# Ordering TensorE's work in the attention loop of a four-layer graph network: row sums behind the counts, transposes and picks later

## The chip, the cores and the metric

The kernel runs on one core of one Trainium2 chip. The metric is the device time of one execution in microseconds. The core's engines work at the same time, each through its own queue in order: TensorE (PE; its weight loads stand apart as PEld), VectorE (DVE), ScalarE (ACT), GpSimd (POOL) and SyncE (SP). They wait for one another by semaphores only.

## What is computed

A graph of 3125 nodes with 64 features and 100000 edges sorted by destination goes through four layers, each added to its input and normalised. The change touches the first, a graph attention over 8 relations:

```python
def _gat_relation(x, src, dst, mask, N, Wr, a_src, a_dst, br):
    h = x @ Wr
    s = h @ a_src
    d = h @ a_dst
    e = jax.nn.leaky_relu(s[src] + d[dst], negative_slope=NEG_SLOPE)
    e = jnp.where(mask, e, -jnp.inf)
    m = jax.ops.segment_max(e, dst, num_segments=N)
    w = jnp.where(mask, jnp.exp(e - m[dst]), 0.0)
    denom = jax.ops.segment_sum(w, dst, num_segments=N)
    alpha = w / denom[dst]
    msg = alpha[:, None] * h[src]
    return jax.ops.segment_sum(msg, dst, num_segments=N) + br
```

The other three layers (degree-normalised sums, three message steps, an edge network) run behind it and are not changed.

## The kernel before

The attention takes the sorted edges in visits of 128 edges. A visit serves one group of 16 nodes, that is 128 (node, relation) pairs. Eight visits (`B`) make a batch, and `NB0` = 122 batches the stage. Each engine runs a `step(n)` for each batch, unrolled by 6 (`RING`) inside a loop (`turns`), and in one step it works on several batches: `n.has(d)` guards the work on batch n+d.

In step n, for each batch concerned:

- SyncE loads the records of batch n+4, and GpSimd gathers the table rows of the batch's source nodes with eight indirect DMAs (line 828). The gather of batch n waits for `hw_ready` of batch n-6, because there are six buffers.
- VectorE (from line 995 on) reduces the transposed scores of batch n to their maxima (`top`, line 1023), makes the masked scores `far` of batch n+1 (line 1031, needs the gathered rows and the `hit` activations of batch n-1), does a chain of small operations, builds the one-hot operands of batch n+2 (lines 1092 to 1101), and then interleaves three things: eight updates of the accumulator with the row sums of batch n-2 (line 1012), eight one-hot `pair_hot` operations for batch n+2 (line 1004, the last sets `hot_ready`), and the weighted rows `hw` of batch n-1 (line 1122).
- TensorE carries a running count table into PSUM (`carries`, line 957, two matmuls) and then adds eight visits to it one after the other (`counts`, line 966, called counts 0 to 7 here). Each count may start only when ScalarE has copied the table as the visit before left it. Between the counts stand the rest of TensorE's work: eight row sums of batch n-2 (`gather_sums`, line 938, two passes each in float32), eight transposes of `far` of batch n+1 (`scores`, line 911) and eight small matmuls that pick values for batch n (`picks`, line 924).
- ScalarE copies each count to SBUF (`keep`, line 864, keeps 0 to 7), and between the copies computes `weight` of batch n-1 (line 878), `fade` of batch n (line 887), the two halves of `hit` for batch n (`hits`, line 856) and the two halves of `hit_t` for batch n+1 (`turned`, line 846). Behind keep 7 it issues the store of the eight copies (line 869).

The order on each engine is written out by hand in its `step`. So TensorE and ScalarE hand a table back and forth eight times a batch, in one PSUM bank: a count, its keep, the next count.

Of the kernel before, what the change touches and what calls it, by code (L numbers as in the profile page):

```python
# [6 lines left out]
ACT = mybir.ActivationFunctionType  # L7
# [695 lines left out]
def attention(nc, k):  # L703
# [5 lines left out]
    with Stage(nc) as c:  # L709
# [6 lines left out]
        def sem(name):  # L716
# [21 lines left out]
        fade_in = sb("fade_in", [P, 2, B])  # L738
        fade = sb("fade", [P, 3, B])
# [15 lines left out]
        hit_ready, hit_t_ready, fade_asked, fade_ready = (sem("hit_ready"), sem("hit_t_ready"), sem("fade_asked"),  # L755
                                                          sem("fade_ready"))
# [79 lines left out]
        @block.scalar  # L836
        def _(act):
            a = nc.scalar

            def turned(n, d, h):  # L840

                s, half = (n.o + d) % 2, slice(4 * h, 4 * h + 4)
                act.wait_ge(masked_ready, n(2, 2 * d + h + 1))
                if h == 0 and n.after(2 - d):
                    act.wait_ge(picked_ready, n(1, d - 1))
                a.activation(hit_t[:, s, half], masked[:, half], ACT.Identity, bias=k.ones_f[:, 0:1],
                             scale=1.0 / BIG).then_inc(hit_t_ready, 1)

            def hits(n, h):

                s, half = n.o % 2, slice(4 * h, 4 * h + 4)
                if h == 0:
                    act.wait_ge(far_ready, n(1, 1))
                    if n.after(2):
                        act.wait_ge(sums_ready, n(1, -1))
                a.activation(hit[:, s, half], far[:, s, half], ACT.Identity, bias=k.ones_f[:, 0:1],
                             scale=1.0 / BIG).then_inc(hit_ready, 1)

            def keep(n, d, i):

                if i == 0 and n.after(2 - d):
                    act.wait_ge(count_written[(n.o + d) % 2], n.pairs(d) * 16)
                act.wait_ge(near_ready, n(B, d * B + i + 1))
                a.copy(count[:, (n.o + d) % 2, i, 0:AW], near[:, (n.o + d) % 2, 0:AW]).then_inc(count_ready, 1)  # L864

            def store(n, d):

                act.wait_ge(count_ready, n(B, d * B + B))
                act.dma_start(k.slots[:, bass.ds(n(B, d * B), B), :], count[:, (n.o + d) % 2, 0:B]
                              ).then_inc(count_written[(n.o + d) % 2], 16)  # L870

            def step(n):
                if n.has(1):
                    keep(n, 1, 0)
                    keep(n, 1, 1)
                if n.has(-1):
                    act.wait_ge(weight_asked, n(1))
                    a.activation(weight[:, (n.o + 1) % 2], lz[:, (n.o + 1) % 2], ACT.Exp).then_inc(weight_ready, 1)
                if n.has(1):
                    keep(n, 1, 2)  # L880
                if n.has(0):
                    hits(n, 0)
                if n.has(1):
                    keep(n, 1, 3)
                if n.has(0):
                    act.wait_ge(fade_asked, n(1, 1))
                    a.activation(fade[:, n.o % 3], fade_in[:, n.o % 2], ACT.Exp).then_inc(fade_ready, 1)
                if n.has(1):
                    keep(n, 1, 4)
                if n.has(0):  # L890
                    hits(n, 1)
                if n.has(1):
                    keep(n, 1, 5)
                    turned(n, 1, 0)
                    keep(n, 1, 6)
                    turned(n, 1, 1)
                    keep(n, 1, 7)
                    store(n, 1)

            turns(act, -1, step)  # L900

        @block.tensor
        def _(pe):
            def scores(n, d, h):

                if h == 0:
                    pe.wait_ge(far_ready, n(1, d + 1))
                    if n.after(1 - d):
                        pe.wait_ge(top_ready, n(1, d))
                for u in range(4 * h, 4 * h + 4):  # L910
                    t = pe.transpose(masked[:, u, :], far[:, (n.o + d) % 2, u, :], k.ident[:])  # L911
                t.then_inc(masked_ready, 1)

            def picks(n, h):

                s = n.o % 2
                if h == 0:
                    pe.wait_ge(pick_ready, n(1, 1))
                    pe.wait_ge(hit_t_ready, n(2, 2))
                    if n.after(1):  # L920

                        pe.wait_ge(zed_taken, n(1))
                for u in range(4 * h, 4 * h + 4):
                    m = pe.matmul(picked[:, 6 * u:6 * u + 6], hit_t[:, s, u, :], pick[:, s, :, u], start=True, stop=True)
                if h == 1:
                    m.then_inc(picked_ready, 1)

            def gather_sums(n, d, h):

                s = (n.o + d) % 2  # L930
                if h == 0:
                    pe.wait_ge(hw_ready, n(1, d + 1))
                    pe.wait_ge(hit_ready, n(2, 2 * d + 2))
                    if n.after(1 - d):

                        pe.wait_ge(acc_step, n(B, d * B))
                for u in range(4 * h, 4 * h + 4):
                    m = pe.matmul(sums[:, u // 4, (u % 4) * TW:(u % 4 + 1) * TW], hit[:, s, u, :], hw[:, s, u, :],  # L938
                                  start=True, stop=True)
                if h == 1:  # L940
                    m.then_inc(sums_ready, 1)

            def carries(n, d):

                s, past = (n.o + d) % 2, (n.o + d + 1) % 2
                _, at = nc.values_load_multi_w_load_instructions(
                    k.start_row[0:1, bass.ds(n(1, d), 1), 0:2].rearrange("a p c -> a (p c)"),
                    engines=[mybir.EngineType.PE], min_val=0, max_val=B,
                    skip_runtime_bounds_check_because="a visit of a batch, or the zeros behind it")
                if n.after(1 - d):  # L950
                    pe.wait_ge(count_ready, n(B, d * B))
                    if n.after(2 - d):
                        pe.wait_ge(deg_added, n(1, d - 1))
                else:
                    pe.wait_ge(run_start, 5)
                for i in range(2):
                    pe.matmul(near[:, s, 0:SW], k.carry_by[:, i, :],
                              count[:, past, bass.ds(at[i], 1), :].rearrange("p i c -> p (i c)"), start=(i == 0), stop=False)

            def counts(n, d, i):  # L960

                s = (n.o + d) % 2
                if i:

                    pe.wait_ge(count_ready, n(B, d * B + i))
                pe.matmul(near[:, s, 0:SW], low_hot[:, s, i, :], pair_hot[:, s, i, :], start=False,  # L966
                          stop=True, skip_group_check=(i > 0)).then_inc(near_ready, 1)

            def step(n):
                if n.has(1):  # L970
                    carries(n, 1)
                    pe.wait_ge(hot_ready, n(1, 2))
                    counts(n, 1, 0)
                if n.has(-2):
                    gather_sums(n, -2, 0)
                if n.has(1):
                    counts(n, 1, 1)
                if n.has(-2):
                    gather_sums(n, -2, 1)
                if n.has(1):  # L980
                    counts(n, 1, 2)
                    scores(n, 1, 0)
                    counts(n, 1, 3)
                    scores(n, 1, 1)
                    counts(n, 1, 4)
                if n.has(0):
                    picks(n, 0)
                if n.has(1):
                    counts(n, 1, 5)
                if n.has(0):  # L990
                    picks(n, 1)
                if n.has(1):
                    counts(n, 1, 6)
                    counts(n, 1, 7)

            turns(pe, -1, step)

        @block.vector
# [696 lines left out]
def keep(nc, k):  # L1695

    with Stage(nc) as c:
        kept = c.semaphore("kept")
        block = c.enter_context(nc.Block())

        @block.vector
        def _(dve):
            nc.vector.tensor_copy(k.x_skip[:], k.x_n[:]).then_inc(kept, 1)
            dve.wait_ge(kept, 1)
# [637 lines left out]
```

## Time and profile before

| | |
|---|---|
| median of 3 runs | 4369.33 us (4359.36 to 4374.9) |
| the profiled execution | 4391.71 us, its span 4390.0 us |
| attention, first `top` to last `top` | 274.8 to 2005.0 us |
| busy over the whole span | PE 67%, PEld 46%, DVE 59%, ACT 34%, POOL 55% |

The page of the profile gives busy tenths of each engine in 40 slices of 110 us; slices 3 to 18 are the attention. Groups of instructions stand by line, engine and operation, with their busy time and with the idle time of the engine before them, together with what ended it. A timeline lists instructions in order of start. "Issue" and "remote" in brackets name idle time for which the profile shows no engine that ended it.

### The profile page before, as it was taken

To read this page: it belongs to the slowest core of one execution; us is meant where nothing else is said; L and a number is where in the kernel's file an instruction comes from. 1 tells how busy PE (TensorE), PEld (TensorE's weight loads), DVE (VectorE), ACT (ScalarE), POOL (GpSimd) and SP (SyncE) were. 2 spreads that over 40 slices of the span, in tenths; PEclk is the share of its full clock that TensorE was granted. 3 is DMA by queue.
4 is the path that set the end of the run, shared out by engine and by line. 5 is a ranking of instruction groups with operands and counts; after the bars stand their busy time and mean duration, and the time that the engine had idled before them with its cause. 6 is when DMAs were issued, how large, how long until landed. Compare 5 with 4: busy or idle time off the path is not lost. (4 is left out here: it accounts for less than half of the span.)

```text
span 4390.0 us, 76379 instructions
## 1 busy us (share of the span) xinstructions
PE 2941.5 (67%) x16134; PEld 2027.4 (46%) x16135; DVE 2594.5 (59%) x9305; ACT 1475.1 (34%) x3181; POOL 2417.1 (55%) x1836
## 2 busy tenths in 40 slices
PE   1636666666666666656567785887878878778762
PEld 0324544444444454443232332666656666666541
DVE  6148888888888887776954443444344443444422
ACT  0124444444444444443010000443333333333320
POOL 0056666666666666550000000588888888888881
PEclk9955555555555555556778876888988989899876
DMA  1353333333333333782603230455555555555543
GB/s 43 100 125 98 97 95 102 97 97 108 90 97 97 106 98 89 86 103 98 169 25 86 71 93 4 47 54 54 53 54 53 54 54 53 54 54 53 54 43 74
DMA packets 654307, 338.20 MB, mean 77 GB/s; under 512 B 437168, under 2 KB 614627, under 8 KB 653284
## 3 DMA queue, kind: packets, MB, share of 16 engines
q0 software_dynamic: 148736, 86.57, 20.5%
q1 hardware_dynamic: 487814, 143.62, 15.5%
q10 hardware_dynamic: 17568, 106.20, 6.0%
q14 instruction: 157, 1.29, 0.1%
q8 instruction: 32, 0.52, 0.1%
HBM read 158.05 MB, written 202.84 MB: 82 GB/s over the span
## 5 line engine op out<-in xcount | busy, mean ns | idle before, releaser
L1847 POOL DMA_INDIRECT sums<-el_rows,el_idx x816 | 1269.2, 1555 | 782.2 <-DVE el_rows L2061 533.9
L828 POOL DMA_INDIRECT at_hs<-table,at_rec_s x976 | 1140.3, 1168 | 614.9 <-DVE at_hw L1122 310.3
L966 PE MATMUL near_ps<-at_pair_hot,at_src_low_hot 128*128 128x425 f16 x976 | 507.4, 520 | 580.1 <-ACT at_count_s L864 319.8
L864 ACT CAST at_count_s<-near_ps 128x400 f16<-128x400 f32 x976 | 481.9, 494 | 987.5 <-PE near_ps L966 446.0
L2059 DVE CAST el_idx<-el_place 128x4 uint32<-128x4 f32 x204 | 35.3, 173 | 840.6 <-DMA sums<-el_rows,el_idx 791.8
L938 PEld LDWEIGHTS sums_ps<-at_hw,at_hit 128*128 128x128 f32 x1952 | 472.9, 334 | 36.3 <-issue 31.7
L966 PEld LDWEIGHTS near_ps<-at_pair_hot,at_src_low_hot 128*128 128x128 f16 x976 | 135.4, 139 | 722.8 <-ACT at_count_s L864 397.9
L938 PE MATMUL sums_ps<-at_hw,at_hit 128*128 128x66 f32 x1952 | 442.2, 408 | 8.7 <-DVE acc L1012 8.7
L1409 PE MATMUL sum_total<-chunk,sum_parts 128*128 128x512 f16 (+1 forms) x700 | 264.2, 391 | 119.9 <-DVE chunk L1511 98.3
L1004 DVE TENSOR_SCALAR at_pair_hot<-iota_wide,at_rec_s 128x400 f16<-128x400 f16 x976 | 324.7, 335 | 0.0
L1995 ACT ACTIVATE el_h<-el_h_ps,el_valid 128x128 f32<-128x128 f32 x816 | 232.6, 368 | 239.3 <-PE el_h_ps L1909 175.8
L1012 DVE SCALAR_TENSOR_TENSOR acc<-acc,at_fade,sums_ps 128x66 f32 x976 | 269.4, 276 | 68.6 <-remote 42.0
L1511 DVE SCALAR_TENSOR_TENSOR chunk<-chunk,minus_past 128x400 f16<-128x400 f16 x464 | 254.3, 625 | 88.0 <-DMA chunk<-slots 88.0
L1863 PE MATMUL el_miss_t<-ident_b,el_miss 128*128 128x128 bf16 x816 | 83.9, 264 | 305.1 <-DVE el_miss L2033 305.1
L1023 DVE TENSOR_REDUCE at_top<-masked 128x8 f32<-128x1024 f32 x122 | 149.1, 1222 | 221.4 <-issue 137.0
L1411 PE MATMUL sum_total<-chunk,sum_parts 128*128 128x512 f16 (+1 forms) x700 | 262.6, 388 | 0.0
L911 PE MATMUL masked<-ident,at_far 128*128 128x128 f32 x976 | 248.6, 407 | 2.7 <-DVE at_far L1031 1.9
L1920 PE MATMUL el_sum_ps<-el_h,el_join 128*128 128x128 f32 x1632 | 245.0, 298 | 7.4 <-DVE el_rows L2061 4.9
L1985 ACT ACTIVATE el_h<-el_h_ps,b 128x512 f32<-128x512 f32 x204 | 140.2, 687 | 318.4 <-PE el_h_ps L1898 264.9
L1031 DVE SCALAR_TENSOR_TENSOR at_far<-at_miss,at_hs 128x1024 f32<-128x1024 f16 x122 | 240.3, 1970 | 0.0
L1909 PE MATMUL el_h_ps<-w,el_h 128*128 128x128 f32 x1632 | 237.3, 289 | 0.0
L1895 PE MATMUL el_h_ps<-el_ea_t,w1b 64*128 64x512 f32 x408 | 235.0, 656 | 0.2 <-issue 0.2
(339 smaller groups left out, 5095.2 us busy)
## 6 DMA issues: line engine op xcount, KB each, us to landing
slots<-at_count_s ACTq DMA_DIRECT2D x122, 850.0 KB
chunk<-slots SPq DMA_DIRECT2D x480, 100.0 KB
el_rec<-attr SPq DMA_DIRECT2D x816, 32.0 KB
attr<-in_edge_attr SPq DMA_DIRECT2D x19, 1248.0 KB
at_rec_s<-meta SPq DMA_DIRECT2D x992, 3.5 KB
at_hs<-table,at_rec_s POOLq DMA_INDIRECT x976
el_pair<-meta SPq DMA_DIRECT2D x816, 1.0 KB
sums<-el_rows,el_idx POOLq DMA_INDIRECT x816
```

Source lines behind the costliest of these rows:

```text
L828: pool.indirect_dma_start(hs[:, s, u, :], None, k.table, bass.IndirectOffsetOnAxis(rec[:, s, u, 0:1].bitcast(U32), 0)).then_inc(gathered[s ...
L864: a.copy(count[:, (n.o + d) % 2, i, 0:AW], near[:, (n.o + d) % 2, 0:AW]).then_inc(count_ready, 1)
L911: t = pe.transpose(masked[:, u, :], far[:, (n.o + d) % 2, u, :], k.ident[:])
L938: m = pe.matmul(sums[:, u // 4, (u % 4) * TW:(u % 4 + 1) * TW], hit[:, s, u, :], hw[:, s, u, :], start=True, stop=True)
L966: pe.matmul(near[:, s, 0:SW], low_hot[:, s, i, :], pair_hot[:, s, i, :], start=False, stop=True, skip_group_check=(i > 0)).then_inc(near_r ...
L1004: return v.tensor_scalar(pair_hot[:, (n.o + d) % 2, u, 0:AW], k.iota_wide[:], rec[:, (n.o + d) % RING, u, 5:6], None, ALU.is_equal)
L1012: v.scalar_tensor_tensor(a, a, fade[:, (n.o + d) % 3, u:u + 1], sums[:, u // 4, (u % 4) * TW:(u % 4 + 1) * TW], ALU.mult, ALU.add).then_in ...
L1409: pe.matmul(first, parts[:, t, 0:2, :].rearrange("p i d -> p (i d)"), near, start=(t == 0), stop=(degree and t == NT - 1))
L1411: m = pe.matmul(second, parts[:, t, 2:4, :].rearrange("p i d -> p (i d)"), near, start=(degree and t == 0), stop=(t == NT - 1))
L1511: ins = v.scalar_tensor_tensor(at, k.chunk[:, q % HELD, g - 1, :], k.minus_past[:, q * CG + g - 1:q * CG + g], at, ALU.mult, ALU.add)
L1847: pool.indirect_dma_start(k.sums_flat[a], bass.IndirectOffsetOnAxis(idx[:, j, a:a + 1], 0), rows[:, j, a, :], None, compute_op=ALU.add).th ...
L1920: m = pe.matmul(sum_ps[:, j % 2, u * P:(u + 1) * P], join[:, s, 4 * h + u, :], h2[:, j % 2, u, :], start=True, stop=True)
```

## The change

Only the orders written out by hand in the attention's TensorE and ScalarE steps change; no instruction is added or removed. On TensorE the eight row sums, formerly four behind count 0 and four behind count 1, stand two behind each of counts 0 to 3. The two halves of the transposes, formerly behind counts 2 and 3, stand behind counts 4 and 5; the two halves of the picks, formerly behind counts 4 and 5, stand behind counts 6 and 7. On ScalarE keeps 0 to 3 come in a row, then `weight`, keep 4, the first half of `hit`, keep 5, the first half of `hit_t`, keep 6, its second half, keep 7 and the store; the second half of `hit` and `fade` come last, behind the store.

```diff
@@ ScalarE
             def step(n):
                 if n.has(1):
-                    keep(n, 1, 0)
-                    keep(n, 1, 1)
+                    for i in range(4):
+                        keep(n, 1, i)
                 if n.has(-1):
                     act.wait_ge(weight_asked, n(1))
                     a.activation(weight[:, (n.o + 1) % 2], lz[:, (n.o + 1) % 2], ACT.Exp).then_inc(weight_ready, 1)
                 if n.has(1):
-                    keep(n, 1, 2)
+                    keep(n, 1, 4)
                 if n.has(0):
                     hits(n, 0)
-                if n.has(1):
-                    keep(n, 1, 3)
-                if n.has(0):
-                    act.wait_ge(fade_asked, n(1, 1))
-                    a.activation(fade[:, n.o % 3], fade_in[:, n.o % 2], ACT.Exp).then_inc(fade_ready, 1)
-                if n.has(1):
-                    keep(n, 1, 4)
-                if n.has(0):
-                    hits(n, 1)
                 if n.has(1):
                     keep(n, 1, 5)
                     turned(n, 1, 0)
...
                     turned(n, 1, 1)
                     keep(n, 1, 7)
                     store(n, 1)
+                if n.has(0):
+                    hits(n, 1)
+                    act.wait_ge(fade_asked, n(1, 1))
+                    a.activation(fade[:, n.o % 3], fade_in[:, n.o % 2], ACT.Exp).then_inc(fade_ready, 1)
@@ TensorE
-                for u in range(4 * h, 4 * h + 4):
+                for u in range(2 * h, 2 * h + 2):
                     m = pe.matmul(sums[:, u // 4, (u % 4) * TW:(u % 4 + 1) * TW], hit[:, s, u, :], hw[:, s, u, :],
                                   start=True, stop=True)
-                if h == 1:
+                if h == 3:
                     m.then_inc(sums_ready, 1)
...
-                if n.has(-2):
-                    gather_sums(n, -2, 0)
+                for h in range(4):
+                    if n.has(-2):
+                        gather_sums(n, -2, h)
+                    if n.has(1):
+                        counts(n, 1, h + 1)
                 if n.has(1):
-                    counts(n, 1, 1)
-                if n.has(-2):
-                    gather_sums(n, -2, 1)
-                if n.has(1):
-                    counts(n, 1, 2)
                     scores(n, 1, 0)
-                    counts(n, 1, 3)
+                    counts(n, 1, 5)
                     scores(n, 1, 1)
-                    counts(n, 1, 4)
+                    counts(n, 1, 6)
                 if n.has(0):
                     picks(n, 0)
                 if n.has(1):
-                    counts(n, 1, 5)
+                    counts(n, 1, 7)
                 if n.has(0):
                     picks(n, 1)
-                if n.has(1):
-                    counts(n, 1, 6)
-                    counts(n, 1, 7)
```

## Rows read from the trace of the kernel before

**Rows 1.** The page's 40 slices of the span: busy tenths, and the granted clock in tenths.
```profile
DVE  6148888888888887776954443444344443444422
ACT  0124444444444444443010000443333333333320
POOL 0056666666666666550000000588888888888881
PEclk9955555555555555556778876888988989899876
```

**Rows 2.** Line 1023 up to 1840 us: count, min/median/max ns, first and last start.
```profile
L1023 DVE TENSOR_REDUCE at_top<-masked x111: 1203/1225/1226, 274.8 to 1832.7; 128x8 f32<-128x1024 f32 x111
```

**Rows 3.** Timeline of one step: start us, us, engine, line, operation, [idle before <-releaser].
```profile
839.03 1.23 DVE L1023 TENSOR_REDUCE at_top<-masked 128x8 f32<-128x1024 f32 x1 [2.31 <-issue]
...
840.29 0.56 PE L966 MATMUL near_ps<-at_pair_hot,at_src_low_hot 128*128 128x425 f16 x1
...
840.65 1.81 PE L938 MATMUL sums_ps<-at_hw,at_hit 128*128 128x66 f32 x8
840.89 0.50 ACT L864 CAST at_count_s<-near_ps 128x400 f16<-128x400 f32 x1 [1.43 <-issue]
...
842.25 0.56 PE L966 MATMUL near_ps<-at_pair_hot,at_src_low_hot 128*128 128x425 f16 x1
...
845.42 0.56 PE L966 MATMUL near_ps<-at_pair_hot,at_src_low_hot 128*128 128x425 f16 x1
...
846.63 0.56 PE L966 MATMUL near_ps<-at_pair_hot,at_src_low_hot 128*128 128x425 f16 x1
846.69 0.28 DVE L1012 SCALAR_TENSOR_TENSOR acc<-acc,at_fade,sums_ps 128x66 f32 x1
...
847.63 0.49 ACT L864 CAST at_count_s<-near_ps 128x400 f16<-128x400 f32 x1 [1.01 <-PE near_ps L966]
...
850.14 0.50 ACT L864 CAST at_count_s<-near_ps 128x400 f16<-128x400 f32 x1
...
850.51 0.71 ACT L846 ACTIVATE at_hit_t<-masked,ones_f 128x512 bf16<-128x512 f32 x1
...
850.69 0.54 PE L966 MATMUL near_ps<-at_pair_hot,at_src_low_hot 128*128 128x425 f16 x1 [0.62 <-ACT at_count_s L864]
851.27 0.49 ACT L864 CAST at_count_s<-near_ps 128x400 f16<-128x400 f32 x1
...
851.91 0.36 ACTq L869 DMA_DIRECT2D slots<-at_count_s  x1
...
852.59 0.56 PE L966 MATMUL near_ps<-at_pair_hot,at_src_low_hot 128*128 128x425 f16 x1
```

**Rows 4.** Timeline of VectorE over one step in which it never waits.
```profile
1631.55 1.23 DVE L1023 TENSOR_REDUCE at_top<-masked 128x8 f32<-128x1024 f32 x1 [2.52 <-issue]
...
1642.95 0.43 DVE L1004 TENSOR_SCALAR at_pair_hot<-iota_wide,at_rec_s 128x400 f16<-128x400 f16 x1
1643.29 1.20 DVE L1023 TENSOR_REDUCE at_top<-masked 128x8 f32<-128x1024 f32 x1
```

**Rows 5.** Timeline around one long idle time of ScalarE between a count and its keep.
```profile
997.60 0.56 PE L966 MATMUL near_ps<-at_pair_hot,at_src_low_hot 128*128 128x425 f16 x1
...
1002.02 0.49 ACT L864 CAST at_count_s<-near_ps 128x400 f16<-128x400 f32 x1 [4.83 <-remote]
```

**Rows 6.** Waits, 800 to 1600 us: waiter <- releaser: us in total, times, longest.
```profile
POOL at_hs L828 <- DVE at_hw L1122: 137.7, 44, 7.4
ACT at_count_s L864 <- remote: 136.2, 35, 6.1
...
DVE acc L1012 <- remote: 21.1, 17, 2.9
```

**Rows 7.** GpSimd's gathers: their group, 800 to 1600 us (busy us, mean ns | idle), and one from the timeline.
```profile
L828 POOL DMA_INDIRECT at_hs<-table,at_rec_s x452 | 533.5, 1180 | 267.9 <-DVE at_hw L1122 137.7 <-issue 130.2
...
840.61 2.38 POOL L828 DMA_INDIRECT at_hs<-table,at_rec_s  x1 [0.30 <-issue]
```

## The prediction

> **What bounds the kernel now.** I read the slices first. In slices 3 to 18, the attention, no engine is full: VectorE stands at eight tenths, ScalarE at four, GpSimd at six, with TensorE's clock mostly near its lower level of 1.2 GHz [rows 1]. A loop in which nobody is full is bound by a hand-over, so the next question is how long a step lasts and who waits in it. The starts of `top` give the step: 110 steps from 274.8 to 1832.7 us, 14.16 us each [rows 2]. The last eleven, up to 2005.0, are slower still (15.7 us each), and I claim nothing there.
>
> What a step could last on VectorE alone is seen where it never waits: from 1631.55 to the next `top` at 1643.29 are 11.74 us [rows 4]. So on average 2.4 us of a step are VectorE waiting. For whom? The timeline of an ordinary step shows the loop between TensorE and ScalarE [rows 3]. From count 0 of one batch (840.29) to count 0 of the next (852.59) it takes 12.30 us and is closed: count, keep, next count, and after keep 7 the carry and count 0 again. Its parts are uneven. Count 0 to keep 0 takes 0.60 (840.29 to 840.89), and a keep to the next count 0.55 (850.14 to 850.69), so a link costs 1.15 where nothing else stands in it. But count 1 comes 1.96 behind count 0 (842.25 against 840.29), because four row sums of two passes fill the 1.81 us between them, and TensorE takes its queue in order. Count 2 is another 1.96 behind, for the same reason. Counts 2 to 4 are 1.21 apart (845.42 to 846.63), counts 4 to 7 together take 4.06 (846.63 to 850.69), and count 7 to the next count 0 takes 1.90.
>
> The second thing in the loop is ScalarE standing still. In 800 to 1600 us, 56.5 steps, it was idle before a keep 35 times with no engine named as releaser, 136.2 us in all [rows 6], 3.9 us each and 0.62 a step. In the one shown, the count began at 997.60, its keep was due at 998.20 and came at 1002.02 [rows 5]: 3.8 us lost. As part of such idle time is ordinary waiting, I take 3.3 us for an average one. Nothing in the chain hides it today: 12.30 + 0.62 x 3.3 = 14.35, against 14.16 measured. That sum is my test that the chain is what sets the step.
>
> **The change, part by part.** *Row sums.* Eight sums stay eight, at about 0.45 us each (four in 1.81). Two behind a count take 0.9, which together with the count's own 0.35 (840.29 to the first sum at 840.65) makes 1.25 at most; by the starts, four sums and a count take 1.96, so two take 1.96 - 0.84 = 1.12. ScalarE's link of 1.15 runs at the same time. So four gaps of 1.15 (at most 1.25) replace 1.96 + 1.96 + 1.21 + 1.21: 4.6 for 6.34, a gain of 1.7 us.
>
> *Transposes.* A count with four transposes is the 1.21 gap seen above. They move to gaps 4 to 5 and 5 to 6: 2.42. *Picks.* These are short and lie within a link: gap 6 to 7 is 1.15, and the second half lies behind count 7, beside keep 7. So counts 4 to 7 take 3.57 instead of 4.06; half a microsecond of that 4.06 is keep 4, which came 1.00 behind its count and not 0.60, and I do not count on that being gone.
>
> *The new closed loop* is 4.6 + 2.42 + 1.15 + 1.90 = 10.07 us, below VectorE's 11.74. So VectorE becomes the pace, and what matters is how much slack ScalarE and TensorE have within 11.74. Let `top` start at T. VectorE's last `pair_hot` ends 0.09 behind it [rows 4], so count 0 can start at about T + 0.2 (it was 1.26). Count 4 follows at T + 4.8, count 6 at T + 7.2. The second `turned` starts 0.95 behind count 6 (0.58 and 0.37) and lasts 0.71: it ends at T + 8.9, and VectorE's next `top`, which waits for it, is due only at T + 11.74. This wait has 2.8 us of slack.
>
> *ScalarE's moved instructions.* `weight` goes from keep 1 to keep 3, about T + 4.7; it is used behind three updates that start at T + 7.66 (846.69), so it costs nothing. `fade` is used two steps later. The second half of `hit` now stands behind the store, with two waits queued ahead of it: ScalarE's wait for keep 7 itself and the issue of the store's DMA. Keep 7 is at T + 8.95; the store is issued 0.64 behind it and takes 0.36 [rows 3]; `hit` then lasts to about T + 10.7. It is not on the way of the sums of two steps later, but VectorE's next `far` waits for it, at T + 11.74 + 1.23. That slack is 2.2 us, smaller than the 2.8 above, so it is the one that counts. SyncE's and GpSimd's queues have nothing moved; the store goes out earlier in the step, in no queue of theirs.
>
> *Sums and updates.* The sums now end behind count 3, near T + 5.0, instead of about T + 5.4. The updates want them at T + 7.66. But the sums now hang on keeps 0 to 2, which they formerly did only for keep 0, so ScalarE's idle time reaches VectorE this way too, with 2.6 us of slack.
>
> *What is left of the idle times.* One of 3.3 us against 2.2 us of slack shows 1.1 us: 0.62 x 1.1 = 0.7 a step. Two within a step or in neighbouring ones share one slack, and keeps late by 0.4 us eat into it; the trace of before cannot show how often this meets, so it is bounded by nothing (0) and by the whole second one (0.62 x 0.62 x 2.2 = 0.85). I take 0.35. The step becomes 11.74 + 0.7 + 0.35 = 12.8 us.
>
> **The sum.** (14.16 - 12.8) x 110 steps = 150 us. The profiled execution took 4391.7 us, so it would have been 4242. The median of the runs is 4369.3, 22 us below the profiled one; the gain is of steps, so it is the same there: 4219 us.
>
> **Rivals.** *The floor.* If the idle times were fully hidden, or TensorE's clock rose with its denser work and shortened the links, the pace would be VectorE's or GpSimd's. A gather takes 1.18 us and 0.30 between two [rows 7], eight 11.8 us a batch: about the same as 11.74. A step of 11.9 gives 2.26 x 110 = 249 us less: 4120. For it: 2.2 us of slack is much, and GpSimd still waits for VectorE, 137.7 us in 56 steps [rows 6]. Against: two engines at their limit, each waiting for the other, seldom reach it.
>
> *Half the gain.* ScalarE's idle times fall before keeps 0 to 2 or behind keep 7 and show nearly in full, and small late keeps recur in the row of four: a step of 13.5, 73 us less, 4296. VectorE's own unexplained idle time before the updates (21.1 us, 17 times, [rows 6]) belongs here.
>
> *No change.* ScalarE's idle times are 23 us apart. If they are paced by time or by how far ScalarE has run ahead, and not by its instructions, a quicker loop only makes them longer, and the step stays near 14.2: 4369. Against this stand steps of 11.74 us without any [rows 4]. The Trainium skill (Runtime: NRT & Kernel Launch, Instruction fetch mechanics) says that a taken branch to a page not held forces a fetch before execution goes on; by that rule idle times go with the code, which has the same length after the change, and the trace here shows no fetch beside them that would prove it.
>
> *Slower.* GpSimd becomes the bound at more than 14.16 us a batch. The gather at 840.61 took 2.38 us [rows 7] while VectorE's `far` ran, against a mean of 1.18. If VectorE's denser work stretched the mean over 14.16 / 8 - 0.30 = 1.47 us, the kernel would be slower than before; at 1.55 a step is 14.8, 70 us more, 4439. Against: a batch of gathers meets one step's operations of VectorE, however fast the steps are. [...]
>
> **Chances.** Forecast 0.47 (4170 to 4260), floor 0.19, half 0.18, no change 0.08, slower 0.08. Within 0.3%, 13 us, a measurement cannot tell this kernel from the one before. Faster by more than that 0.84, the same 0.08, slower 0.08. The range from 4110 to 4320 takes in the floor, the forecast and the half.
>
> **What would show it.** In the profile after: counts 0 to 4 at 1.15 us from one to the next; sums in pairs; `top` starting mostly with no idle time before it; VectorE at nine tenths in the attention's slices; GpSimd's 137.7 us of waiting for `hw` much reduced; and idle time of VectorE before `far` (line 1031) and the updates (line 1012), where formerly there was next to none before `far`. I am wrong if the gaps between counts 0 and 4 stay near 2 us, if ScalarE's idle times grow beyond 0.62 a step or 3.9 us, or if a gather's mean goes well over 1.18.

## The result and the profile after

The changed kernel was slower: 4431.14 us in the median (4413.78 to 4456.59, 4 runs) against 4372.11 (4359.36 to 4379.41) for the kernel before on the same chip, a ratio of 1.0143 with a 95% interval of 1.0086 to 1.0199. The forecast was 4219. The profiled execution took 4456.59 us, its span 4454.9; that of before took 4391.71. Medians and ratios here and below leave out a run more than 1.5% above the fastest of its kernel, which were two: one of `act_only` (5203 us) and one of `pe_load_late` (6000 us).

The slices of the changed kernel's page, which answer to [rows 1]; the attention is slices 3 to 18 or 19:

```profile
PE   1635655565556565546477876777878777787862
ACT  0124444444444444433100000333333334333320
DVE  6147887788878787777766334534344444444432
POOL 0065665666656665651000000488888888888881
PEclk9856566555655655566688776788898889899886
```

VectorE is no fuller than before (seven to eight tenths, where nine were forecast), and the attention reaches a slice further. The row of `top` answers to [rows 2] (count, min/median/max ns, first and last start):

```profile
L1013 DVE TENSOR_REDUCE at_top<-masked x108: 1204/1210/1225, 274.3 to 1856.1; 128x8 f32<-128x1024 f32 x108
```

That is 1581.8 us over 107 steps, 14.8 each, against 14.16. The last `top` of all starts at 2068 instead of 2005.0 us, 63 us later; the spans differ by 64.9. So nearly all of the loss is in the attention's steps.

Did the new order do what it says? The counts of one clean step of the changed kernel (start us, us, engine, line, operation, [idle before <-releaser]):

```profile
864.81 0.54 PE L961 MATMUL near_ps<-at_pair_hot,at_src_low_hot 128*128 128x425 f16 x1 [1.69 <-DVE at_pair_hot L994]
...
865.93 0.54 PE L961 MATMUL near_ps<-at_pair_hot,at_src_low_hot 128*128 128x425 f16 x1
...
869.30 0.54 PE L961 MATMUL near_ps<-at_pair_hot,at_src_low_hot 128*128 128x425 f16 x1
```

Count 1 is 1.12 us behind count 0 and count 4 is 4.49 behind it, as the working had it (1.15 and 4.6), where the old order needs 6.3. Over all steps of this trace, clean or not, the median from count 0 to count 4 is 6.10 us, against 6.74 in the trace of before. The gaps of a clean step came out right and the time did not; and count 0 had waited for VectorE, of which more below. The waits of 800 to 1600 us, for [rows 6], say where it went (waiter <- releaser: us in total, times, longest):

```profile
ACT at_count_s L864 <- remote: 243.4, 74, 6.8
POOL at_hs L828 <- DVE at_hw L1112: 175.7, 31, 12.7
...
DVE acc L1002 <- PE sums_ps L933: 55.4, 18, 6.9
...
DVE at_top L1013 <- issue: 31.5, 11, 5.2
...
DVE at_far L1021 <- issue: 19.9, 10, 7.3
...
DVE at_far L1021 <- ACT at_hit L856: 6.8, 3, 5.8
```

The idle times before a keep that have no engine as releaser went from 35 to 74, from 136.2 to 243.4 us, that is from 0.62 to 1.37 a step, the prediction's own sign of being wrong. And VectorE, which in the old order waited only before `top` and a little before the updates, now waits for the sums (55.4 us) and before `far` (26.7 us). GpSimd's wait for `hw` rose, where it should have fallen. The gathers themselves did not lengthen:

```profile
L828 POOL DMA_INDIRECT at_hs<-table,at_rec_s x432 | 501.7, 1161 | 302.6 <-DVE at_hw L1112 175.7 <-issue 126.9
```

A mean of 1161 ns, against 1180 [rows 7], ends the rival in which GpSimd is the bound. What is left is ScalarE "standing still", and there the trace says more than the waits do. Its record of the semaphore that a count raises and a keep waits for shows the increment itself coming late: as a rule 0.55 to 0.58 us behind the count's start, but in these cases only 0.02 us before the keep begins. Two of them in one stretch of the changed kernel, the second with the row sums that stand behind it in TensorE's queue:

```profile
1097.42 0.56 PE L961 MATMUL near_ps<-at_pair_hot,at_src_low_hot 128*128 128x425 f16 x1
...
1101.14 0.95 POOL L828 DMA_INDIRECT at_hs<-table,at_rec_s  x1 [0.30 <-issue]
1101.95 0.50 ACT L864 CAST at_count_s<-near_ps 128x400 f16<-128x400 f32 x1 [3.98 <-remote]
...
1102.50 0.53 PE L961 MATMUL near_ps<-at_pair_hot,at_src_low_hot 128*128 128x425 f16 x1 [3.76 <-issue]
...
1102.83 0.95 PE L933 MATMUL sums_ps<-at_hw,at_hit 128*128 128x66 f32 x4
...
1106.15 1.18 POOL L828 DMA_INDIRECT at_hs<-table,at_rec_s  x1 [0.30 <-issue]
1107.09 0.49 ACT L864 CAST at_count_s<-near_ps 128x400 f16<-128x400 f32 x1 [4.65 <-remote]
```

Count 1 started at 1102.50, its increment is recorded at 1107.07, 4.57 us later, and ScalarE copied at once. ScalarE was not slow, it had not been told; nor was TensorE, which began the sums behind the count at 1102.83. The same lateness is in TensorE's increments for the transposes, the picks and the sums, but in none of those that are recorded of ScalarE's copies. Recorded is the word: where increments come late, many have no record at all. Of ScalarE's 976 copies 615 have one in the kernel before and 558 in the changed one, where the undisturbed traces further down have over 920. So lateness is counted here by the keeps' starts.

The late ones come in steps: about 1.1, 1.8, 2.5, 3.2, 3.9, 4.6 us behind the usual time, 0.7 apart, up to 7.4. In the changed kernel three in four lie within 0.12 us of such a step, in the kernel before only half. They come only while GpSimd is working through its gathers. Of the counts of before that fell more than 2.6 us after the last gather had started, 0 of 128 were late, of the others 115 of 736; of after, 0 of 197 and 188 of 667. (`act_only`, below, has the one exception, 1 of 172.) In the same traces some register instructions of SyncE's queue take 0.7 us instead of 0.037. From here on a "late keep" is one that starts more than 0.9 us after it was due, that is after 0.56 us from its count's start or the end of ScalarE's instruction before it. The figure given is their total over six steps, one turn of the loop: 15.7 us in the kernel before, 26.5 in the changed one.

### The profile page after: what moved, and what is told of

Same layout as the page of the kernel before. It is cut to its first block and busy times, and to the rows that moved or that the text cites. A ratio compares the mean times of both kernels' runs of the same rounds, so it can differ in the third digit from the quotient of the medians.

```text
span 4454.9 us, 76379 instructions
## 1 busy us (share of the span) xinstructions
PE 2856.1 (64%) x16134; PEld 2009.0 (45%) x16135; DVE 2592.7 (58%) x9305; ACT 1479.7 (33%) x3181; POOL 2406.6 (54%) x1836
## 3 DMA queue, kind: packets, MB, share of 16 engines
q1 hardware_dynamic: 487814, 143.62, 15.2%
## 5 line engine op out<-in xcount | busy, mean ns | idle before, releaser
L828 POOL DMA_INDIRECT at_hs<-table,at_rec_s x976 | 1128.6, 1156 | 698.5 <-DVE at_hw L1112 370.7
L961 PE MATMUL near_ps<-at_pair_hot,at_src_low_hot 128*128 128x425 f16 x976 | 492.0, 504 | 625.7 <-issue 307.1
L933 PEld LDWEIGHTS sums_ps<-at_hw,at_hit 128*128 128x128 f32 x1952 | 489.3, 312 | 32.5 <-issue 23.4
L961 PEld LDWEIGHTS near_ps<-at_pair_hot,at_src_low_hot 128*128 128x128 f16 x976 | 102.0, 104 | 752.6 <-issue 345.1
L2033 DVE SCALAR_TENSOR_TENSOR el_join<-el_src_t,el_ends,tri 128x128 f32<-128x128 f32 x816 | 228.7, 346 | 2.1 <-PE el_src_t L1859 2.1
```

Of the source, the lines that this page charges most:

```text
L828: pool.indirect_dma_start(hs[:, s, u, :], None, k.table, bass.IndirectOffsetOnAxis(rec[:, s, u, 0:1].bitcast(U32), 0)).then_inc(gathered[s ...
```

## The experiments

The runs came in five series, each on one chip with the kernel before beside it. They fall into two kinds, and nothing in what follows can be understood without that. The kernel before took:

| series | kernel before, us | late keeps in the series' traces |
|---|---|---|
| the result above | 4372 | yes |
| 1 | 4373 | yes |
| 2 | 4195 | none |
| 3 (the chip of series 2 again) | 4337 | yes |
| 4 | 4203 | none |
| 5 | 4193 | none |

So a kernel is compared with the kernel before of its own series only. The expectations name their theories by letters of their own.

**Series 1: which engine's order, and what makes the increments late.** `pe_only` has TensorE's new order with ScalarE's old one, `act_only` the reverse:

> TensorE's new order with ScalarE's old one. Theory T (TensorE's semaphore increments for its counts arrive late, and do so the more often the denser the counts follow each other and the more of them fall right behind the start of a step): the counts 0 to 4 come 1.15 us apart where nothing is late, the late keeps rise as in the changed kernel (some 26 us in six steps against 16), and the time is near 4430, at least 4400. Rival R (the loss is ScalarE's: the second half of hit behind the store holds far, line 1031, and with it VectorE): ScalarE's old order takes that away, and the time is under 4330.

> ScalarE's new order with TensorE's old one: keeps 1 to 3 wait behind the row sums as before. Theory T: late keeps stay near 16 us in six steps; the time is 4350 to 4400, the same as before within 0.7%. Rival R (the loss is in ScalarE's order): slower than before by 50 us or more.

`pe_only` took 4397.1 us, a ratio of 1.005 (1.0026 to 1.0074), `act_only` 4426.3, a ratio of 1.0124 (1.0072 to 1.0176). Their late keeps were 15.2 and 20.5 us. Neither half gives a gain alone. Theory T missed twice: it wanted some 26 us of late keeps and at least 4400 us from `pe_only`, and no more late keeps than before from `act_only`. Rival R missed `pe_only` (under 4330) and had the size of `act_only`'s loss (50 us or more). With TensorE's order alone VectorE waited 1.2 us a step for sums that hang on keeps 0 to 2 (0.4 before the updates in the kernel before), and 0.7 instead of 1.7 before `top`; its profiled run took 4392.2 us, level with the profiled 4391.7 of before, so the trace can't say where its half per cent comes from. ScalarE's order alone brings the wait before `far` (0.38 a step).

`no_gather` is the changed kernel with the table rows gathered for the first six batches only (the waits for gathers are eased to fit, which is not shown), `no_load` with the records loaded for the first six only. So both work on old rows. The excerpt is from `no_gather`:

```diff
...
-                if not n.has(0):
+                if not n.has(0) or n.o >= RING:
                     return
                 s = n.o % RING
                 pool.wait_ge(rec_loaded[s], (n.round(0) + 1) * (16 * B))
...
```

> The changed kernel in which GpSimd gathers the table rows of the first six batches only; the rows of all later batches are left out (the buffers keep old rows). If the late increments come from traffic of the gathers (theory T1: their DMAs' descriptors and semaphore increments), late keeps fall from 26 us in six steps to under 8 and a step of the attention lasts 11.8 us, so the kernel takes about 4090. If they come from TensorE itself (rival T2: its passes, its queue or its code), they stay over 20 us in six steps and the kernel stays over 4350.

> The changed kernel in which SyncE loads the records of the first six batches only; all later record loads are left out (the buffers keep old records, so the gathers repeat old rows). Theory T3 (the eight small loads a batch on SyncE's queue delay the increments): late keeps fall under 8 us in six steps and the kernel takes about 4090. T1 or T2: late keeps stay over 20 us in six steps and the time stays within 2% of 4431.

`no_gather` took 4113.2 us, with 0.0 us of late keeps and a mean step of 12.1 us; `no_load` took 4255.1, with 14.4 us of them still, which is neither the under 8 us of theory T3 nor the over 20 of its rivals. Each is one run. By them the lateness needs GpSimd's gathers and does not need SyncE's loads, though fewer loads lessen it. SyncE's register instructions of 0.7 us went with it: 71 of 591 between 400 and 1500 us in the changed kernel, none of 725 without gathers.

**Series 2: remedies, where nothing was wrong.** `sums_pairs` takes only the sums' part of the change, pairs behind counts 0 to 3, all else as before. `load_late` is the changed kernel and `pe_load_late` is `pe_only`, both with SyncE's loads waiting for the picks instead of `hot_ready`. `b_no_gather` is the kernel before without gathers behind the first six batches.

```diff
-sp.wait_ge(hot_ready, n(1, d + 1 - RING))
+sp.wait_ge(picked_ready, n(1, 1))
```

> The kernel before (old order) in which GpSimd gathers the rows of the first six batches only. It gives the old order's step without late increments. Theory A (without GpSimd's gathers no increment is late, in whatever order, and the new order's chain is really shorter): no late keeps, a step at the larger of VectorE's 11.7 and the old chain's 11.6 to 12.3, so 11.7 to 12.3 us, against 11.6 (median) of the new order without gathers; time 4110 to 4180. Theory B (the new order is slower for a reason of its own): this kernel is faster than the changed one without gathers (4113) by 20 us or more.

> One part alone: the row sums in pairs behind counts 0 to 3, transposes, picks and ScalarE's order as before. Theory A (lateness grows with how many of TensorE's increments fall in GpSimd's active time soon after each other, and the more of them at the step's start): 1.3 us a step shorter chain, late keeps between 16 and 22 us in six steps, time 4340 to 4400. Rival (the cost is in the picks behind count 7 or the transposes behind count 4): this part alone is faster than before by 40 us or more.

> The changed kernel, in which SyncE issues the record loads of batch n+4 only when TensorE's picks of step n are done, that is behind count 7, and not at the start of the step. Theory C (gathers and record loads together on the way of the increments; without loads the lateness was 14 us in six steps, with them 26): late keeps fall to 14 to 19 us in six steps and the time to 4260 to 4350, faster than both kernels. Rival (the loads matter only through their own number, wherever they stand): late keeps stay near 26 and the time near 4430.

> TensorE's new order with ScalarE's old one, and the record loads behind the picks as in load_late. Theory C: late keeps fall from 15 us in six steps to under 12, time 4270 to 4350. Rival: stays at 4397 within 0.5%.

They took 4138.3, 4173.4 (0.9953; 0.9936 to 0.9969), 4191.0 (0.9991; 0.9981 to 1.0) and 4183.6 us (0.9982; 0.997 to 0.9995), and none had a late keep. It looked as if the later loads had cured it, but `sums_pairs`, which has the old loads, had none either, and the kernel before stood at 4195 us instead of 4373. So what was expected of the last three, which rests on late keeps, stayed untried. `b_no_gather` lies within theory A's 4110 to 4180 and not below the changed kernel without gathers (4113), so theory B falls. The series tells nothing of the cure; what it tells is that the late increments are a matter of the occasion, and that without them the order hardly moves the time.

**Series 3: the same kernels where increments are late.** By luck it was the chip of series 2, so a lasting property of a chip isn't the cause.

> The kernel before, unchanged, for its trace on the chip of this call. Theory D (late increments of TensorE are a property of the chip: some have them, some have none, with the same program): either a time near 4372 with about 16 us of late keeps in six steps, or a time near 4195 with none and a step of the attention of about 12.4 us; nothing between. Rival (the lateness varies from run to run on any chip): values between the two.

> The changed kernel, unchanged. Theory D: if the chip has the late increments, 1.01 times the kernel before, as recorded. If it has none, the change does what its chain says: VectorE sets the step (11.74 us), the old order's excess of about 0.6 us a step goes, and the kernel is faster than before by 0.3 to 1.2%: 4145 to 4182 against 4195. Rival (the new order is slower for a reason of its own): 1.01 times the kernel before here too.

> Only the row sums in pairs. Without late increments: 0.995 times before, as measured. With late increments: its counts fall in the same phase as before except the first three, so late keeps of 15 to 20 us in six steps and 0.99 to 1.01 times before.

> The changed kernel with SyncE's record loads behind the picks. Without late increments: 0.999 times before, as measured. With late increments: late keeps fall from 26 us in six steps to 14 to 19, and the time to 4260 to 4350 against 4372.

| | us | ratio (95%) | late keeps, six steps | mean step |
|---|---|---|---|---|
| `before_again` | 4344.9 | one run | 12.7 | 13.84 |
| `after_again` | 4343.7 | 1.0025 (0.9999 to 1.0051) | 19.1 | 13.91 |
| `sums_pairs_again` | 4340.9 | 1.0013 (0.9995 to 1.0031) | 5.0 | 13.69 |
| `load_late_again` | 4385.8 | 1.0102 (1.0056 to 1.0148) | 22.2 | 14.18 |

The loads' move is a miss: it made things worse than the kernel before, and its late keeps did not fall. The changed kernel was level here and 1.4% slower in the first series, so how much it loses also depends on the occasion; but in both it has half as much again of late keeps or more (19.1 to 12.7; 26.5 to 15.7). `sums_pairs_again` had few late keeps, where 15 to 20 us were expected, and hardly gained by it: its step is 13.69. There 58 of the transposes' recorded increments came over 1 us late, against 32 in `before_again`, and VectorE's wait before the updates rose from 0.20 to 0.73 us a step.

**Series 4: what the order is worth undisturbed.** Here increments came in time by themselves. `after_third` is the changed kernel; `a_no_gather` and `b_no_gather_2` are the two kernels without gathers, side by side; `hits_back` is the changed kernel with one part undone:

```diff
                     keep(n, 1, 5)
+                if n.has(0):
+                    hits(n, 1)
+                if n.has(1):
                     turned(n, 1, 0)
...
                 if n.has(0):
-                    hits(n, 1)
                     act.wait_ge(fade_asked, n(1, 1))
```

> The changed kernel unaltered, once more. On both earlier occasions TensorE's increments came late and it gave 1.014 and 1.0025 of the kernel before. Theory L (late increments take the gain): if there are none here (0 late keeps, the kernel before near 4195 us), it gives 0.995 to 1.000 of the kernel before, as its load_late form did (0.999), and a median step near 11.75 us; if there are, 1.000 to 1.015 again, with 19 us or more of late keeps per six steps. Rival O (the new order itself costs time, by its sums and its hit activations): 1.005 or more in either case.

> The changed kernel with the table rows gathered for the first six batches only (its values are then those of the first six batches); as before under the label no_gather, now timed beside the same edit of the kernel before on the same chip. Theory L: no late keeps, mean step 12.1 us, and 10 to 30 us faster than b_no_gather_2, which is what the new order is worth where no increment is late. Rival O: not faster than b_no_gather_2.

> The kernel before with the table rows gathered for the first six batches only. Both theories: no late keeps, mean step 12.3 us (4138 us where no increment was late). Theory L: a_no_gather lies 10 to 30 us lower. Rival O: a_no_gather lies level with it or higher.

> The changed kernel with one part undone: the second half of hit stands behind keep 5 and not behind the store. Theory L: VectorE's wait before far falls below 0.1 us a step (0.4 to 0.6 in the changed kernel), the late keeps remain, and the time falls by 0.2 to 0.5 us a step, 20 to 50 us, against after_third where increments come late, and by under 10 us where they don't. Rival (the far wait only stands in for the next wait, top or updates, which grows by as much): within 10 us of after_third in either case.

`after_third` took 4182.8 us against 4203.0, a ratio of 0.9948 (0.9932 to 0.9965): faster by half a per cent. `a_no_gather` took 4113.6 and `b_no_gather_2` 4138.9, 25 us apart; each had four runs and they don't overlap (4109.5 to 4116.0, 4136.5 to 4142.8). Theory L's expectations of these three came out, and O falls: the order by itself costs nothing. `hits_back` took 4185.4 (0.9958; 0.9944 to 0.9972), level with `after_third`; VectorE's wait before `far` was nil in both, so its part in the disturbed loss stays untried.

**Series 5: the kernel before undisturbed.**

> The kernel before unaltered, for its profile. If no increment of TensorE comes late (its time near 4200 us), Theory L wants five of six steps at VectorE's 11.7 us and the sixth, with the loop's jump, near 15.6 us, a mean of 12.3 to 12.4 us, no late keep, and counts 0 to 4 in 6.3 us all the same: the old order's uneven gaps then cost nothing. A chain of TensorE and ScalarE that sets the step, as the prediction has it, wants no step under 12.3 us. If increments come late, a mean of 13.8 us and 12 us or more of late keeps per six steps, as in before_again.

> The changed kernel with four of the eight gathers of a batch (the values of four visits of each batch are then old ones). If late keeps go with GpSimd's gathers in progress and increments come late at all on this occasion: half of the 19 to 26 us per six steps, 8 to 14 us, and a mean step of 13.0 to 13.5 us. If any gather at all is enough: 19 us or more. If none comes late: a mean step of 12.3 us, and it tells nothing of this.

`before_third` took 4195.2 us, as theory L wanted: five steps in six near 11.7 us, the sixth near 16.1 (15.6 expected), a mean of 12.46. `half_gather` took 4127.7 with no late keep, so, as nothing was late in the series, it says nothing on whether half the gathers would make half of the lateness. The profile of `before_third` is the one that the prediction lacked. TensorE's clock doesn't explain the difference: between 400 and 1500 us the granted clock was 0.56 of full speed in the profile of before and 0.60 after, and 0.60 in `before_third` and 0.63 in `after_third`, with a median count of 537 to 539 ns in all four. So the clock did rise with the new order, and no count became shorter. Its waits, 800 to 1600 us:

```profile
ACT at_count_s L864 <- PE near_ps L966: 252.1, 193, 2.4
...
PEld near_ps L966 <- DVE at_pair_hot L1004: 60.0, 64, 1.3
...
DVE at_top L1023 <- issue: 41.5, 10, 4.4
...
POOL at_hs L828 <- DVE at_hw L1122: 32.8, 10, 3.9
```

And those of `after_third`:

```profile
ACT at_count_s L864 <- PE near_ps L961: 294.3, 314, 2.7
PEld near_ps L961 <- DVE at_pair_hot L994: 170.0, 65, 3.1
...
DVE at_top L1013 <- issue: 37.0, 11, 8.8
...
POOL at_hs L828 <- DVE at_hw L1112: 17.9, 10, 2.4
```

No line ends in "remote" in either. In the old order the weight load of count 0 waits for VectorE's `pair_hot` in every one of 64 steps, and the matmul itself 0.34 us a step; in the new order the matmul waits 2.2 us:

```profile
PE near_ps L966 <- DVE at_pair_hot L1004: 21.9, 44, 0.7
```

(21.9 / 64) in `before_third`, and

```profile
PE near_ps L961 <- DVE at_pair_hot L994: 144.0, 65, 2.6
```

(144.0 / 65) in `after_third`. So the loop between TensorE and ScalarE closes before VectorE is ready, even with the old order. Counts 0 to 4 took 6.31 us and now take 4.49, 1.8 less, and the wait grew by 1.9: all that the row sums gave turned into waiting. In both kernels five steps in six last less than 12 us, with medians of 11.71 and 11.73, VectorE's own time [rows 4]. VectorE was the pace already.

What, then, are the 20 us that the new order does gain? They are in one step in six, the one with the loop's jump: about 16.1 us in `before_third`, 14.9 in `after_third`. VectorE's jump in `before_third`, with the store (ACTq) beside it:

```profile
857.52 0.34 ACTq L869 DMA_DIRECT2D slots<-at_count_s  x1
...
858.11 0.32 DVE L1004 TENSOR_SCALAR at_pair_hot<-iota_wide,at_rec_s 128x400 f16<-128x400 f16 x1
...
862.83 1.22 DVE L1023 TENSOR_REDUCE at_top<-masked 128x8 f32<-128x1024 f32 x1 [4.41 <-issue]
```

and in `after_third`:

```profile
849.08 0.34 ACTq L869 DMA_DIRECT2D slots<-at_count_s  x1
...
851.96 0.32 DVE L994 TENSOR_SCALAR at_pair_hot<-iota_wide,at_rec_s 128x400 f16<-128x400 f16 x1
...
855.12 1.23 DVE L1013 TENSOR_REDUCE at_top<-masked 128x8 f32<-128x1024 f32 x1 [2.85 <-issue]
```

In the old order the store goes out 0.6 us before VectorE's last instruction of the turn, in the new one 2.9 us before it. The queues of the two microseconds behind that instruction (packets, MB, share of 16 engines), first `before_third`, 858.4 to 860.4 us:

```profile
q10 hardware_dynamic: 126, 0.86, 104.0%
q0 software_dynamic: 17, 0.00, 1.0%
```

then `after_third`, 852.3 to 854.3:

```profile
q0 software_dynamic: 87, 0.08, 23.2%
q1 hardware_dynamic: 288, 0.01, 7.6%
q14 instruction: 1, 0.01, 1.3%
```

q10 carries the store, q14 code. In the old order the store fills all sixteen DMA engines in these two microseconds, and the packet of code comes behind it, 1.9 to 2.4 us after VectorE's last instruction; in the new order it comes after 0.6 to 1.2. From that packet to `top` it is 2.0 us in both, so all of the difference lies ahead of it. The mean of VectorE's idle time at the 16 jumps before 1550 us follows that in seven kernels: with the store issued just ahead, 4.17 (`before_third`) and 3.98 (`b_no_gather_2`); with it 2.1 to 2.6 us ahead, 3.29 (`hits_back`), 3.10 (`load_late`), 2.85 (`after_third`) and 2.74 (`a_no_gather`); and 2.66 in `sums_pairs`, whose store's packets start only 0.6 us behind the packet of code, and whose counts 0 to 4 are no closer than before (6.8 us). That last one is telling: it has the whole gain (0.9953) without any shorter chain. With some 19 turns, 1.3 us each make 25 us, the size of the gain. `pe_load_late` has the short idle time too (2.7) and gained only 0.2%: to the 108th `top` it is 21 us ahead of `before_third`, in the last 14 steps it loses 12 of them. No run moved the store alone, so the cause rests on these traces and not on an edit of its own. The Trainium skill (Runtime: NRT & Kernel Launch, Instruction fetch mechanics) has a taken branch to a page that isn't held wait for a fetch; the code packet in each of these idle times agrees.

## Why the prediction was wrong

**The gaps between the counts: right.** 1.12 us for a forecast 1.15, 4.49 for 4.6; counts 0 to 4 became 1.8 us shorter, where 1.7 were worked out.

**VectorE's own step: right.** 11.71 to 11.73 us in the median undisturbed, for 11.74.

**What the old order's step is made of: wrong, and this step failed.** The prediction took the loop of one timeline, 12.30 us [rows 3], added 0.62 idle times of 3.3 us, met the 14.16 of [rows 2] within 0.2, and took that as its test. The sum was right by accident. The 12.30 had small delays in it (4.06 us for counts 4 to 7, where `before_third` has 3.1 in the median), and the loop closes 0.3 us inside VectorE's 11.7. So without idle times the old order also runs at VectorE's pace (mean step 12.46 with the jumps), and of the 1.36 us a step that were forecast the order had none to give there. The other term was mis-sized too: the idle times with no releaser are only part of the late keeps, of which there were 1.07 a step of 2.45 us, 2.6 us a step, for the 0.62 of 3.3, 2.05 us. A sum that meets the mean doesn't show that its terms lie in a row; the wait of count 0 on `pair_hot` would have, but in the disturbed profile it is rare (7 of 57 steps in `before_again`).

**The idle times: the wrong owner.** They were called ScalarE's standing still, and held unchanged in number and size. Their size held: 2.4 to 2.5 us for a late keep in both kernels of the first series. Their number didn't: 6.4 per six steps became 10.6, and 6.3 became 9.4 in series 3. They are increments of TensorE's, so they strike its sums and transposes too. The rival "no change", at 8 in 100, came nearest: it had the idle times grow with a quicker loop, but by their length, and only enough to eat up the gain. "Slower", the way it went, also had 8 in 100, for a reason that did not come true.

**The slack: there, and too small for the number.** By the 12.46 and 12.26 us of the undisturbed runs the disturbance costs the old order 1.7 us a step (14.14) of 2.6 us of late keeps in the profile of before (15.7 / 6), and the new order 2.65 (14.91) of 4.4 (26.5 / 6). Hidden are 0.9 and 1.8 us a step. So the slack took in twice as much, as far as late keeps alone can tell (late sums are not in them), and the additional lateness took all of it and more: (14.91 - 14.14) x 104 = 80 us between the fourth and the 108th `top`, of which the first three steps, 12 us quicker in the changed run, give back a part; the spans are 65 apart.

**The new places where VectorE waits: foreseen, priced too low.** The sums behind keeps 0 to 2, with "2.6 us of slack", were named and given no price of their own; they cost 55.4 us of 800. `far` behind `hit` behind the store cost 26.7.

**GpSimd as the bound: rightly put low**; its gathers held their mean of 1.16 to 1.18 us. Those with `far` beside them for the whole of their usual 0.94 us took 2.38 us in the median in both kernels, about one in nine of 976, so denser work on VectorE did not bring more of them. It takes part in another way: next to nothing is late while it idles.

**Open.** Why the new order draws more late increments. Within GpSimd's gathers 16% of the old order's counts were late and 28% of the new one's in the first profiles, 14% and 23% in series 3. In the new order most of the excess is at counts 0 and 7 (6.7 and 5.6 us per six steps, formerly 2.1 and 0.2), those at the two ends of the gathers' row. That shift comes with TensorE's order: `pe_only` has 4.3 and 4.3 there, but less at counts 2 and 6, and the same total (15.2). `act_only` has the higher total (20.5) by count 2 (10.0 for 5.2). So both orders have a part. What carries a semaphore's increment, and why TensorE's are late beside GpSimd's gathers and ScalarE's are not, no run shows; nor what decides whether a series has the lateness.

## What to carry to other kernels

A step whose parts add up to its mean isn't yet explained: ask of the first instruction of the loop whom it waits for, and in the fastest steps, not in the average ones. Where several steps already run at the time of one engine without waits (here 13% of them under 12 us in the profile of before, at 11.74), the rest of the mean can be disturbance, as most of it was here, and a new order is worth only what it hides of that, less what it adds. And an idle time with no engine as releaser belongs to nobody until the semaphore's own record has been read.

## What the runs showed of the hardware

- Increments of TensorE's semaphores can come 1.1 to 7.4 us late, most clearly in steps of 0.7 us in the changed kernel, while GpSimd is issuing gathers, on some occasions and not on others, on the same chip. Where they do, a third to two fifths or so of the increments of ScalarE's copies have no record. SyncE's queue shows it too. The same register instructions (min/median/max ns), 800 to 1600 us, in the changed kernel:

```profile
L784 SPq FUSED_REGOPS  x432: 3/37/729, 801.6 to 1594.5; - x144
```

and in `before_third`:

```profile
L784 SPq FUSED_REGOPS  x519: 37/37/42, 800.2 to 1598.2; - x173
```

- With it the kernel before took 4337 us where it had taken 4195 on the same chip, 3.4% more, and 4373 on another; the change moves the time by 0.5 to 1.4%. A comparison within one series is needed, and its result holds for that kind of series: the changed kernel is 1.4% slower, level, or 0.5% faster.
- VectorE's jump back costs 2.7 to 4.2 us of idle time; with a store of 0.86 MB issued just ahead of it, it is 1.3 us more than with the store 2.6 us ahead.
